# A two-layer graph kernel on one core: six masks moved into stage one, eight more split adjacency tiles, four column blocks summed in PSUM

## What is computed

```
# layer 0 (W1 128x16, W2 16x128x128, b 16x128)
node = x @ W1
hw   = einsum('nc,kcf->nkf', x, W2)
x0   = einsum('nk,nkf->nf', node, hw)
y    = relu(adj @ x0 + node @ b)
x1   = layernorm(x + y)
# layer 1 (W 128x128, B 128)
msg  = x1 @ W + B
sens = exp(-(1/adj - 1)**2 / (2 * 0.5**2))
w    = where(adj < 1, sens, 0)
out  = layernorm(x1 + w @ msg)
```

## Time and profile before

| | |
|---|---|
| median of 3 runs | 550.95 us (550.93 to 551.05) |
| profiled execution | 552.33 us, of which the span on the core is 550.5 us |
| PE busy | 543.5 us, 99% of the span |
| DVE busy | 497.3 us, 90% |
| ACT busy | 497.2 us, 90% |
| POOL busy | 83.3 us, 15%, all of it in the first 104 us |
| DMA | 142 MB, mean 258 GB/s; 315 GB/s in most of stage two, 399 GB/s between 112 and 128 us |
| TensorE clock | granted 1.00 throughout, which is 2.4 GHz |
| stage one ends | at 102.3 us (first row tile on PE) |
| last row tile ends | near 489 us |

### The profile page before, as it was taken

The page is one execution under the profiler, slowest core; times in us unless marked ns, Lnnn a source line. Parts: engine busy times, 40 slices in busy tenths (PEclk is TensorE's granted clock), DMA queues, the critical chain, the costliest instruction groups (busy, mean ns, idle before and its releaser), DMA issues.

```text
span 550.5 us, 5213 instructions
## 1 busy us (share of the span) xinstructions
PE 543.5 (99%) x1780; PEld 325.7 (59%) x1780; DVE 497.3 (90%) x564; ACT 497.2 (90%) x448; POOL 83.3 (15%) x76
## 2 busy tenths in 40 slices
PE   9999999999999999999999999999999999999996
PEld 7887888655655565556555655565555555554444
DVE  6686777999998799999989999999989998999997
ACT  5777888449999999989999999999999998999984
POOL 2888899400000000000000000000000000000000
PEclk9999999999999999999999999999999999999999
DMA  5992000299997888888888888887988796870003
GB/s 169 394 426 93 21 1 0 78 373 426 414 359 279 319 317 323 311 307 323 331 305 310 326 320 312 314 314 301 329 307 308 301 327 235 314 283 1 0 20 133
DMA packets 23130, 142.05 MB, mean 258 GB/s; under 512 B 2720, under 2 KB 3264, under 8 KB 6720
## 3 DMA queue, kind: packets, MB, share of 16 engines
q1 hardware_dynamic: 22960, 141.46, 68.5%
q10 hardware_dynamic: 144, 0.26, 0.2%
HBM read 139.62 MB, written 2.10 MB: 257 GB/s over the span
## 4 chain that ended last, share of the span: by engine, by line
PE 92%; DMA 4%; POOL 1%; issue 1%; ACT 1%; DVE 1%; DVEq 0%; ACTq 0%; POOLq 0%
PE l_ps L502 26%; PE acc_ps L451 17%; PE kept_ps L502 10%; PE acc_ps L442 6%; PE acc_ps L440 6%; PE acc_ps L441 6%; PE hw_ps L410 4%; DMA x_in<-xT_dram 4%; PE hw_ps L416 4%; PE hw_ps L413 4%; PE acc_ps L502 2%; PE var_ps L483 1%; PE acc_ps L457 1%; PE acc_ps L388 1%; POOL prods L1315 1%
## 5 line engine op out<-in xcount | busy, mean ns | idle before, releaser
L502 PE MATMUL l_ps<-wt_pair,msg 128*128 128x512 f32 x328 | 147.3, 592 | 0.0
L909 DVE SCALAR_TENSOR_TENSOR wt_pair<-wt_pair 128x2048 f32<-128x2048 f32 x60 | 136.5, 2285 | 3.5 <-DMA wt_pair<-adjT_dram 3.5
L616 ACT ACTIVATE wt_pair<-wt_pair 128x4096 f32<-128x4096 f32 (+1 forms) x33 | 109.0, 3302 | 10.9 <-DVE wt_pair L909 10.9
L621 ACT ACTIVATE wt_pair<-wt_pair 128x4096 f32<-128x4096 f32 (+1 forms) x33 | 109.0, 3302 | 0.3
L502 PEld LDWEIGHTS l_ps<-wt_pair,msg 128*128 128x128 f32 x328 | 61.7, 190 | 70.3 <-issue 69.2
L451 PE MATMUL acc_ps<-rows,x 128*128 128x512 f32 x216 | 96.8, 592 | 0.0
L600 ACT ACTIVATE prods<-hw_ps,node 128x128 f32<-128x128 f32 x256 | 73.1, 374 | 17.5 <-PE hw_ps L416 15.7
L897 DVE TENSOR_TENSOR row_lo<-rows,adj_hi 128x2048 fp32r<-128x2048 f32 x37 | 84.8, 2293 | 1.3
L864 DVE SCALAR_TENSOR_TENSOR part_acc<-hw_ps,node,part_acc 128x128 f32<-128x128 f32 x224 | 60.7, 343 | 21.1 <-PE hw_ps L416 21.1
L451 PEld LDWEIGHTS acc_ps<-rows,x 128*128 128x128 f32 x216 | 41.0, 190 | 50.1 <-issue 49.8
L440 PE MATMUL acc_ps<-adj_hi,x_hi 128*128 128x512 f32 x148 | 68.3, 462 | 0.0
(11 more groups left out here) (117 smaller groups left out, 554.7 us busy)
## 6 DMA issues: line engine op xcount, KB each, us to landing
rows<-adjT_dram SPq DMA_DIRECT2D x68, 1024.0 KB, 4.9
wt_pair<-adjT_dram SPq DMA_DIRECT2D x60, 1024.0 KB, 4.8
x_in<-xT_dram SPq DMA_DIRECT2D x8, 256.0 KB, 3.9
x_row<-xT_dram SPq DMA_DIRECT2D x8, 256.0 KB, 5.1
outT_dram<-sumT SPq DMA_DIRECT2D x7, 256.0 KB, 2.0
W_in<-W_dram SPq DMA_DIRECT2D x3, 256.0 KB, 4.5
W_in<-W_dram ACTq DMA_DIRECT2D x1, 256.0 KB, 3.7
outT_dram<-sumT SPq DMA_DIRECT2D x2, 128.0 KB, 1.9
```

The source lines that it names most:

```text
L502: mm = pe.matmul(out, msg[:, c % 2, k, :], wt[t][:, k, :], start=(first and k == 0), stop=(last and k == CH - 1))
L616: act.activation(w, w, ACT.Ln, bias=TINY).then_inc(ln_made, 1)
L621: act.activation(w, w, ACT.Exp, scale=-1.0).then_inc(inv_made, 1)
L909: dve.scalar_tensor_tensor(out=w, in0=w, scalar=1.0, in1=w, op0=ALU.is_lt, op1=ALU.mult).then_inc(made, 1)
```

## The change

- **Splits.** Block g = 6 is split too, in rows 1 to 7, and g = 4 in row 1: 45 split row tiles instead of 37. `x0_lo` of blocks 3, 5 and 7 is written over `x0` itself; blocks 1, 4 and 6 have room apart.
- **Two-pass rows.** ROWS_TWO_PASS is (1, 6) instead of (2, 6).
- **Kept blocks.** The even destination blocks 0, 2, 4, 6 are summed in `kept_ps` (four banks), the odd ones use one bank of `l1_ps` (and `acc_ps` bank 0 from tile 50 on). `add_part` runs 35 times instead of 49. `x1` of an even row is written by `scale_row` straight into `sumT`, so `add_row` is left for rows 1, 3, 5, 7.
- **Banks.** `yc_ps` is gone; `centre(r)` writes over the bank of `acc_ps` that row r used, so row r + 2 waits for `x1_made` of row r instead of `y_made`. `messages(r)` of a two-pass row comes after the column tile of its step instead of before it.
- **First masks.** The first six weight tiles are loaded ahead of the first five row tiles, and `mask(g - 1)` follows `sum_over_k(g)` for g = 1 to 6 on DVE.
- **Lists.** The DVE and ACT lists of stage two are written anew.

```diff
-KEPT = 2
-L1_BANKS = 2
+KEPT = 4
+L1_BANKS = 1
-SPLIT = (1, 3, 4, 5, 7)
-SPLIT_FIRST = ((3, 5, 7), (1, 3, 5, 7))
-SPLIT_LAST = (1, 3, 4, 5, 7)
+SPLIT = (1, 3, 4, 5, 6, 7)
+SPLIT_FIRST = ((3, 5, 7), (1, 3, 4, 5, 6, 7))
+LO_APART = (1, 4, 6)
+SIXTH, SIXTH_ROWS = 6, (2, 3, 4, 5, 6)
+SPLIT_LAST = (1, 3, 4, 5, 6, 7)
-ROWS_TWO_PASS = (2, 6)
+ROWS_TWO_PASS = (1, 6)
...
+    def is_kept(j):
+        return j % 2 == 0
     def is_added(t):
-        return t % NB >= KEPT or t >= TILES - NB
+        return not is_kept(t % NB) or t >= TILES - NB
...
+            for t in range(WT_RING - LATE_SLOTS):
+                load_wt(t)
             for i in range(ROW_RING):
                 load_row_tile(i)
-            for t in range(WT_RING - LATE_SLOTS):
-                load_wt(t)
...
                 if g == 0:
-                    at_least(pe, y_made, r - 1)
+                    at_least(pe, x1_made, r - 1)
...
-                if g == 4 and 1 <= r < NB or i == TILES + 3:
+                if (g == 4 and 1 <= r < NB and not row_in_two_pass(r - 1)) or i == TILES + 3:
                     messages(r - 1)
                 t = i - COL_LAG
                 if t >= 0:
                     col_tile(t)
+                if g == 4 and 1 <= r < NB and row_in_two_pass(r - 1):
+                    messages(r - 1)
...
-            round_x0(NB - 1)
             take_ln(0)
             take_inverse(0)
+            round_x0(NB - 1)
...
-                dve.tensor_tensor(x1T[:, :], yc_ps[:, :], rstd[:, 0, :], ALU.mult).then_inc(x1_made, 1)
+                dve.tensor_tensor(x1T[r], yc_ps[r], rstd[:, 0, :], ALU.mult).then_inc(x1_made, 1)
...
+                if 1 <= g <= FIRST_PAIR:
+                    mask(g - 1)
...
             remainder_of_x0(1)
-            mask(0)
             split_row_tile(7)
-            mask(1)
-            mask(2)
+            remainder_of_x0(4)
+            mask(6)
+            remainder_of_x0(6)
             split_row_tile(9)
             residual(0)
-            mask(3)
+            mask(7)
             split_row_tile(11)
-            mask(4)
-            mask(5)
+            split_row_tile(12)
+            mask(8)
             scale_row(0)
             split_row_tile(13)
-            add_row(0)
-            mask(6)
+            mask(9)
             copy_messages(0)
+            split_row_tile(14)
             split_row_tile(15)
```

More of the change, by code:

```diff
@@ L122, in width, with rows_added @@
         return BW if u < NB - 1 else HALF_BW
+    def is_kept(j):
+        return j % 2 == 0
     def is_added(t):
-        return t % NB >= KEPT or t >= TILES - NB
+        return not is_kept(t % NB) or t >= TILES - NB
     def added_to(t):
         return len([s for s in range(t + 1) if is_added(s)])
+    def rows_added(r):
+        return len([q for q in range(r + 1) if not is_kept(q)])
     def in_two_pass(u):
@@ L134, in row_in_two_pass @@
         return ROWS_TWO_PASS[0] <= r <= ROWS_TWO_PASS[1]
-    shared = [t for t in range(TILES) if t % NB >= KEPT]
+    shared = [t for t in range(TILES) if not is_kept(t % NB)]
     bank_of, before = {}, {}
@@ L156, in sem @@
             return ctx.enter_context(nc.semaphore(name))
[L158 to L161, removed]
+        with ExitStack() as whole:
+            x0 = sb("x0", [P, NB * CH, P], F32, whole)
+        x0_in_place = sb("x0_in_place", [P, NB * CH, P], F32R)
+        x0_hi = sb("x0_hi", [P, len(SPLIT) * CH, P], F32R)
+        x0_apart = sb("x0_apart", [P, len(LO_APART) * CH, P], F32R)
+        x0_lo = {}
+        for g in SPLIT:
+            if g in LO_APART:
+                n = LO_APART.index(g)
+                x0_lo[g] = x0_apart[:, n * CH:(n + 1) * CH, :]
+            else:
+                x0_lo[g] = x0_in_place[:, g * CH:(g + 1) * CH, :]
         sumT = sb("sumT", [P, N])
@@ L204, in gnn_kernel @@
         rstd_rounded = sb("rstd_rounded", [P, 2, BW], F32R)
-        x1T = y
+        x1T = [block_of(sumT, q) if is_kept(q) else y[:, :] for q in range(NB)]
         msg = sb("msg", [P, 2, CH, P])
@@ L489, in col_tile @@
                     pe.wait_ge(msg_copied, c + 1)
-                if j >= KEPT:
+                if not is_kept(j):
                     if before[t] is not None:
@@ L494, in col_tile @@
                     elif t >= THIRD_FROM:
-                        pe.wait_ge(y_made, NB - 1)
+                        pe.wait_ge(x1_made, NB - 1)
                     out, first, last = shared_ps[bank_of[t]], True, True
                 else:
-                    out, first, last = kept_ps[:, j, :], c == 0, c == NB - 1
+                    out, first, last = kept_ps[:, j // 2, :], c == 0, c == NB - 1
                 pe.wait_ge(wts_made, part_of[t] + 1)
@@ L506, in last_col_tile @@
             def last_col_tile(half):
-                pe.wait_ge(sum_added, added_to(before[LAST] if half == 0 else TILES - NB + 1))
+                pe.wait_ge(sum_added, added_to(before[LAST] if half == 0 else TILES - NB + 2))
                 pe.wait_ge(wts_made, part_of[LAST] + 1)
@@ L688, in _ @@
             take_ln(4)
+            square(0)
+            take_inverse(4)
+            log_variance(0)
             take_exp(3)
-            take_inverse(4)
             take_square(4)
+            inverse_root(0)
             take_ln(5)
@@ L1095, in _ @@
             split_row_tile(25)
-            take_square(12)
-            mask(17)
+            add_part(9)
             split_row_tile(27)
             residual(2)
-            add_part(10)
+            mask(17)
             round_row(2)
@@ L1106, in _ @@
             mask(20)
+            take_square(16)
+            round_square(2)
+            mask(21)
+            remainder_of_square(2)
             split_row_tile(28)
-            round_square(2)
-            add_part(12)
-            remainder_of_square(2)
-            mask(21)
-            take_square(16)
             add_part(13)
@@ L1204, in _ @@
             scale_row(5)
-            add_part(38)
+            split_row_tile(54)
+            add_part(39)
             add_row(5)
             copy_messages(5)
+            mask(48)
             split_row_tile(55)
-            add_part(39)
-            mask(48)
+            take_square(44)
             split_row_tile(57)
+            add_part(41)
             mask(49)
-            take_square(44)
+            residual(6)
             mask(50)
-            split_row_tile(59)
-            residual(6)
-            add_part(42)
             round_row(6)
```

327 lines of the change are left out of this document (159 added, 168 removed).

## The result

The changed kernel is slower: **559.1 us** (median of four runs, 556.91 to 561.85) against 551.0 us (550.93 to 551.14), a ratio of 1.0149 with a 95% interval of 1.0104 to 1.0194. The forecast was 545.8 us, the range ended at 554.5 us, and faster had a chance of 0.62.

What follows compares the result with a forecast made beforehand. PE (TensorE), with 92% of the chain, was taken as the bound, DVE as runner-up. 550.5 - 6.4 - 0.7 + 1.5 + 0.4 = 545.3 us of span, 0.45 more for the median: 545.8 us; range over the cases 544.0 to 554.5.

Steps and rivals of the forecast that it cites:

- Stage one, +0.4 us: Masks at block ends in stage one fit DVE's gap; PE late only after block 1, costing 0.4 us.
- if masks in this place run as in stage two: Condition on the stage-one masks: at 2.20 us each they cost PE 0.4 us in all.
- rival 1: Stage one: masks on DVE and POOL's sums exclude each other, stage one grows 8 us, 553.8 us; chance 0.30.
- PE's part, -6.4 us: Stage two: eight more split tiles save 5.6 us on PE, row 1's two-pass products 0.8 us.
- the gone wait at `messages(5)`: Stage two: PE's wait for `scale_row` goes, as `messages(5)` stands a column tile later: -0.7 us.
- DVE's part, +1.5 us of PE's time: Stage two: DVE gets 6.8 us more work and falls short, costing PE 0 to 2.6 us, taken as 1.5.
- `copy_messages(0)` was late behind `mask(9)`: Row 1: mask and copy end half a microsecond after PE wants its first column tile, inside the 1.5 us.
- The fear that a row of 53.5 us on DVE would slow one of 53.4 us on PE: Rows 2 to 6: DVE needs 53.5 us, PE 53.4; each row a tie with no recovery until row 7 ends.
- Loads, ACT, PSUM: no cost: Reordered first loads, ACT's earlier logarithm and the new bank use were each said to cost nothing.
- The sum of stage two: Stage two's terms together, -6.4, -0.7 and +1.5 us: 5.6 us shorter.

Runs made afterwards that it cites:

- one_input: Changed kernel with each of the six stage-one masks replaced by a one-input maximum over the same 2048 columns: 546.07 us, ratio 0.9915.
- masks_short: Changed kernel with its six stage-one masks cut to 64 of 2048 columns: 546.39 us, ratio 0.9893.
- four_in_row_one: Changed kernel without masks in stage one, only row tiles 9, 11, 13, 15 split in row 1, both lists reordered: 548.58 us, ratio 0.9942.
- loads_only: Kernel before with only the first weight tiles loaded ahead of the first row tiles: 552.87 us, ratio 1.0013.
- masks_in_stage_one: Kernel before with the earlier loads and masks 0 to 5 moved into stage one, after blocks 1 to 6: 563.11 us, ratio 1.0212.

## Why the prediction was wrong

**Stage one, +0.4 us: this step failed.** It measured 10.5 us, and up to 4 more in executions in which the clock falls. The reading of the earlier trace rows was right as far as it went: an instruction of 2.28 us on DVE has its place at the end of a block and costs PE 0.15 us, which `one_input` shows. What failed is the premise "if masks in this place run as in stage two". The price was known to have two ends, 0.4 and 8 us, with no row that excluded the upper one, and a rule that named just this pair of instructions; the lower end was taken all the same, and the chances of 0.54 to 0.30 were put on the side for which nothing spoke. The only argument against rival 1 was that no such pair was in the trace, and that is none.

**Rival 1** is what happened. Its chain (sums on POOL, then ACT for the folds, then PE for ACT) stands in the waits line by line. Its price was mis-sized, 8 us for 10.5: I let POOL's slack and ACT's margin take back 5 of 13.2 us, and they took back 2.7. It gave 553.8 us, 5 us under the median. For the traced execution, whose clock is whole, the sum can be compared term by term: the rival's span was 553.3 us and the measured one is 3.3 us longer. Up to rounding, the masks are 2.1 of these (10.5 for 8.4), the slow start less the one wait of before that is gone 0.7, and stage two 0.4. The clock, which it didn't have either, comes on top in the runs at 0.990. A wait of PE was priced at its own length, where getting going again took a quarter more (2.1 us on 8.4); that, the start and the clock are what the upper end of the range lacked.

**PE's part, -6.4 us: right.** A split saved 0.70 us, to the hundredth in the rows of two kernels. With two-pass products in row 1 and the gone wait at `messages(5)`, the six rows from row 2 on (bias to bias, 174.09 to 494.65 us, and 162.57 to 488.83 us before) come to 320.6 us against 326.3: 5.7 us, which is 6 x 0.70 + 0.8 + 0.7.

**DVE's part, +1.5 us of PE's time: right in kind, a little small.** All of it is in row 1. `copy_messages(0)` was late behind `mask(9)` and its tile, as named: 0.82 us for the 0.5 expected; with the 0.20 us at a split ahead of it, and what PE takes to come back into step after each (the products between the two biases need 33.6 us and took 35.3), it is 1.7 us. The tail took 0.2 us more. The fear that a row of 53.5 us on DVE would slow one of 53.4 us on PE for six rows was not borne out in this kernel. It is a near thing, though: `masks_short` lost 1.5 us in row 2 and `four_in_row_one` 1.2 us in row 5.

**Loads, ACT, PSUM: no cost**, as said. `loads_only` shows the first, the logarithm at 114.70 us the second; PE has no wait for a bank in stage two.

**The sum of stage two** was -5.6 us and measured -5.2. Nearly all that is wrong is in the one term of stage one.

## What to carry to other kernels

Before work is moved into an engine's gap, list what runs on the *other* engines in that gap, and count the SBUF inputs of both. A DVE instruction with two of them takes turns with POOL's sums, so it can cost its length on both queues (here 1.75 us of TensorE's time for each 2.28), and POOL, which by its 15% looked the idlest engine of all, had 0.35 us left in a block of 11.83 us in that very stage. A price that no row shows is to be taken where a rule puts it, not where the rows are silent; an instruction of the same length with one input would have told the two apart. A wait of TensorE of 1.7 to 2.7 us is to be priced with what the clock may add behind it, here up to 4.3 us. And where two engines tie in every row, as DVE and PE do here, a forecast should leave room for a lost row: two of the versions lost one, by 1.2 and 1.5 us.

## What the runs showed of the hardware that was not expected

- DVE's work beside POOL's sums, with two inputs in SBUF and with one: the mask as the second to come took 3.90 us instead of 2.28, POOL's three sums 6.71 us instead of 4.59 behind a mask, and a maximum over the same tile took 2.28 us and left POOL's sums at 4.59 us.
- After waits of 1.69 to 2.74 us TensorE was granted the lower of its two levels in some executions and not in others of the same program; with the same wait at 65 us the one lost nothing and the other 4.3 us. The mean clock of a whole run tells the long stretches apart: 0.995 or more against 0.990 or less. A short one hardly shows in it: `masks_in_stage_one` has 0.997.
- The program starts at one of two paces. In some traces (of the changed kernel, `loads_only`, `masks_short` and `one_input`) the products of block 0 start 0.43 us apart until past 9 us, in others (of before, `masks_in_stage_one`, `four_in_row_one` and three more) 0.23 us apart from 6.5 us on. 0.43 us is also their pace behind the wait at 65 us, where the clock shows 0.5; at the start it shows 1.00 at either pace, so the pace has to be read from the products. The two traces of the kernel with three masks are one of each, both with a lower clock behind a wait, and their first row tiles are at 113.1 and 110.9 us; the 2.2 us between them are also about what lies between the two levels of before. What decides the pace is open; the loads don't, since `loads_only` has a trace at the slow pace and four of its ten runs on the lower level.
